# A fused attention and feed-forward layer in fp32: VectorE's sum of two probability tiles moved to another place in the unit, and GpSimd's work reordered

## What is computed

```python
xq = rope(q @ Wq); xk = rope(kv @ Wk); xv = kv @ Wv      # q = kv = layernorm(x)
xk = jnp.repeat(xk, 2, axis=-1); xv = jnp.repeat(xv, 2, axis=-1)
# 16 heads of 64
scores = jax.nn.softmax(xq @ xk * scale, axis=-1)
out = (scores @ xv) @ Wo
ffn = (silu(x @ w_gate.T) * (x @ w_up.T)) @ w_down.T     # x = layernorm(x) here too
x = x + out + ffn
```

## Time and profile before

| | us |
|---|---|
| median of three runs | 1159.65 (1156.83 to 1164.91) |
| the profiled execution | 1166.15 |
| its span, first to last instruction | 1164.4 |

### The profile page before, as it was taken

One profiled execution on the slowest core, in us unless ns is written; L12 is line 12 of the kernel. 1 busy time (PEld: TensorE's weight loads), 2 busy tenths in 40 slices (PEclk: granted clock), 3 DMA queues, 4 the chain that ended last, 5 costly groups with the idle time before them and its releaser, 6 DMA issues.

```text
span 1164.4 us, 17086 instructions
## 1 busy us (share of the span) xinstructions
PE 1120.0 (96%) x6288; PEld 663.2 (57%) x6288; DVE 901.1 (77%) x1023; ACT 729.8 (63%) x1327; POOL 852.9 (73%) x268
## 2 busy tenths in 40 slices
PE   5899899999999999999999999999999999999997
PEld 4787455655565555556565555555555555554443
DVE  7686877787887877788787877778787877776655
ACT  3234666666676666666676666666676666665564
POOL 3222868788788778888788778887778878887660
PEclk9899999999999999999999999999999999998889
DMA  6662908062340718062341718072341618050000
GB/s 230 159 258 77 256 2 224 1 205 58 85 141 19 207 37 224 2 205 57 96 129 26 201 37 224 1 210 53 96 130 30 196 37 224 1 130 1 5 1 19
DMA packets 56338, 124.98 MB, mean 107 GB/s; under 512 B 8000, under 2 KB 19520, under 8 KB 54080
## 3 DMA queue, kind: packets, MB, share of 16 engines
q1 hardware_dynamic: 56256, 123.90, 36.8%
HBM read 53.08 MB, written 10.49 MB: 55 GB/s over the span
## 4 chain that ended last, share of the span: by engine, by line
PE 79%; DVE 14%; SPq 2%; ACT 2%; issue 1%; DMA 1%; POOL 0%; DVEq 0%; ACTq 0%; POOLq 0%
PE bank_o L406 20%; PE bank_s L554 18%; PE scores L391 17%; DVE row_max L946 12%; PE scores L373 7%; PE bank_m L381 3%; PE bank_m L442 2%; PE bank_m L416 2%; PE bank_m L419 2%; SPq L239 2%; PE scores L492 2%; PE bank_s L509 1%; ACT prob L867 1%; PE bank_o L509 1%; DVE stats L961 1%
## 5 line engine op out<-in xcount | busy, mean ns | idle before, releaser
L946 DVE TENSOR_REDUCE row_max<-scores 128x1 f32<-128x1024 f32 x512 | 597.1, 1214 | 206.8 <-PE scores L391 206.5
L867 ACT ACTIVATE prob<-bank_s 128x512 f32<-128x512 f32 x992 | 576.7, 600 | 252.9 <-PE bank_s L554 229.5
L1181 POOL TENSOR_TENSOR prob_sum<-prob_sum,prob 128x2048 f32<-128x2048 f32 x93 | 425.7, 4577 | 13.5 <-ACT prob L867 0.5
L554 PE MATMUL bank_s<-qk_pack 98*128 98x512 f32 x992 | 415.8, 434 | 7.1 <-ACT prob L867 3.1
L391 PE MATMUL scores<-qk_pack 96*128 96x512 f32 x1024 | 337.5, 411 | 8.9 <-DVE row_max L946 0.3
L554 PEld LDWEIGHTS bank_s<-qk_pack 98*128 98x128 f32 x992 | 186.9, 189 | 184.9 <-issue 84.7
L406 PE MATMUL bank_o<-prob,v 128*32 128x512 f32 x2048 | 253.0, 612 | 0.0
L391 PEld LDWEIGHTS scores<-qk_pack 96*128 96x128 f32 x1024 | 179.5, 190 | 74.5 <-DVE row_max L946 53.0
L1181 POOL TENSOR_TENSOR prob_sum<-prob_sum,prob_pair 128x2048 f32<-128x2048 f32 x31 | 142.7, 4602 | 101.7 <-DVE prob_pair L1039 101.7
L1125 POOL TENSOR_TENSOR qk_stage<-rope,qk_stage 128x512 fp32r<-128x512 f32 x64 | 81.8, 1279 | 92.3 <-ACT qk_stage L753 92.3
L1173 POOL TENSOR_TENSOR prob_sum<-prob 128x2048 f32<-128x2048 f32 x31 | 142.2, 4586 | 0.0
(11 more groups left out here) (105 smaller groups left out, 742.4 us busy)
## 6 DMA issues: line engine op xcount, KB each, us to landing
qk_pack<-qk_stage SPq DMA_DIRECT2D x384, 128.0 KB, 5.0
table<-tables SPq DMA_DIRECT2D x16, 2048.0 KB, 9.6
w_stage<-w_scratch SPq DMA_DIRECT2D x14, 640.0 KB, 4.5
v<-v_stage SPq DMA_DIRECT2D x32, 256.0 KB, 8.1
xT_scratch<-xT_hl SPq DMA_DIRECT2D x4, 1024.0 KB, 9.5
x_stage<-xT_scratch SPq DMA_DIRECT2D x4, 1024.0 KB, 7.0
w_scratch<-w_split SPq DMA_DIRECT2D x1, 2560.0 KB, 15.1
x_all<-x SPq DMA_DIRECT2D x4, 512.0 KB, 11.7
```

Source lines behind the costliest of these rows:

```text
L554: mm(bank_s[:, h % 2, :], qk_pack[j][0:SCORE_K, 1, kt // QT, h, (kt % QT) * 128:(kt % QT + 1) * 128], qk_pack[j][0:SCORE_K, 0, t, h, :], s ...
L867: A(prob[:, kt % RING, h, :], bank_s[:, h % 2, :], ACT.Exp).then_inc(prob_ready, 1)
L946: V.tensor_reduce(row_max[:, m:m + 1], scores[:, at:at + 2, :].rearrange("p c k -> p (c k)"), axis=AX.X, op=ALU.max).then_inc(max_read, 1)
L1181: TT(prob_sum[:, t], prob_sum[:, t], part, ALU.add).then_inc(sum_done, 1)
```

## The change

DVE's `pair_sum(u)` now adds key tiles 2 and 3, and stands after maximum tile 11 (`PAIR_AFTER`), that is ahead of tiles 12 to 15, the split and the normalisation, where it stood behind them and ahead of `rotate`. GpSimd's order in a unit is now: first low part, add of 0+1, second low part, output add, then the pair (2+3), 4, 5 and 6. ACT's waits follow from the new readers of the ring: key tiles 6 and 7 wait for the pair, the next unit's key tiles 0, 1 and 2 for the adds of 4, 5 and 6. The arithmetic is the same but for the order of the sums. PE's and SyncE's streams are the same.

```diff
--- before.py
+++ after.py
@@ -70,6 +70,7 @@
 NE = HG
 
 INVERT_AFTER = 9
+PAIR_AFTER = 11
 
 
 def build(nc, x, tables, w_qkv, wo_even, wo_odd, w_gu, w_down, ident_in, out):
@@ -852,16 +853,14 @@
 
                     if not (first and kt < RING):
                         act.wait_ge(pv_done, 8 * u + kt - 3)
-                        if kt < 2:
-                            act.wait_ge(pair_done, u)
-                        elif kt == 2:
-                            act.wait_ge(sum_done, 5 * u)
+                        if kt < 3:
+                            act.wait_ge(sum_done, 5 * u - 2 + kt)
                         elif kt == 3:
                             act.wait_ge(den_ready, u)
                         elif kt < 6:
                             act.wait_ge(sum_done, 5 * u + 1)
                         else:
-                            act.wait_ge(sum_done, 5 * u + kt - 4)
+                            act.wait_ge(pair_done, u + 1)
                     for h in range(HG):
                         act.wait_ge(score_ready, 32 * u + 4 * kt + h + 1)
                         A(prob[:, kt % RING, h, :], bank_s[:, h % 2, :], ACT.Exp).then_inc(prob_ready, 1)
@@ -895,10 +894,8 @@
             def last_slot():
                 for kt in range(KT):
                     act.wait_ge(pv_done, 8 * LAST + kt - 3)
-                    if kt < 2:
-                        act.wait_ge(pair_done, LAST)
-                    elif kt == 2:
-                        act.wait_ge(sum_done, 5 * LAST)
+                    if kt < 3:
+                        act.wait_ge(sum_done, 5 * LAST - 2 + kt)
                     elif kt == 3:
                         act.wait_ge(den_ready, LAST)
                     elif kt < 6:
@@ -1034,9 +1031,9 @@
 
             def pair_sum(u):
 
-                dve.wait_ge(prob_ready, NE * (KT * u + 6))
-                at_least(dve, sum_done, 5 * u - 1)
-                V.tensor_tensor(prob_pair[:], prob[:, 4 % RING], prob[:, 5 % RING], ALU.add).then_inc(pair_done, 1)
+                dve.wait_ge(prob_ready, NE * (KT * u + 4))
+                at_least(dve, sum_done, 5 * u - 3)
+                V.tensor_tensor(prob_pair[:], prob[:, 2], prob[:, 3], ALU.add).then_inc(pair_done, 1)
 
             def invert(u):
                 dve.wait_ge(denT_ready, u + 1)
@@ -1056,12 +1053,14 @@
                         reduce_tile(u + 1, m)
                         if m == INVERT_AFTER and not is_first(u):
                             invert(u - 1)
+                        if m == PAIR_AFTER:
+                            pair_sum(u)
                     split_max(u + 1)
                 else:
                     invert(u - 1)
+                    pair_sum(u)
                 if not is_first(u):
                     normalise(u - 1)
-                pair_sum(u)
                 if not last_pair:
                     rotate(u + 4, t, 2 * i + j + 2)
 
@@ -1119,8 +1118,8 @@
         def _(pool):
             TT = nc.gpsimd.tensor_tensor
 
-            def split_lo(w, t):
-                for k in range(2):
+            def split_lo(w, t, halves=range(2)):
+                for k in halves:
                     pool.wait_ge(hi_done, 2 * w + k + 1)
                     TT(qk_stage[:, 2 * k + 1, t, :], rope[:, 2 * k, :], qk_stage[:, 2 * k, t, :].bitcast(F32), ALU.subtract).then_inc(lo_done, 1)
 
@@ -1166,18 +1165,21 @@
 
             pool.wait_ge(filled, 3)
 
-            def add_probs(u, t):
+            def add_first(u, t):
 
                 at_least(pool, den_ready, u - 1)
                 pool.wait_ge(prob_ready, NE * (KT * u + 2))
                 TT(prob_sum[:, t], prob[:, 0], prob[:, 1], ALU.add).then_inc(sum_done, 1)
-                for n, kt in enumerate((2, 3, 4, 6)):
-                    if kt == 4:
+
+            def add_rest(u, t):
+
+                for n, kt in enumerate((2, 4, 5, 6)):
+                    if kt == 2:
                         pool.wait_ge(pair_done, u + 1)
                     else:
                         pool.wait_ge(prob_ready, NE * (KT * u + kt + 1))
                     pool.wait_ge(sum_done, 5 * u + n + 1)
-                    part = prob_pair[:] if kt == 4 else prob[:, kt % RING]
+                    part = prob_pair[:] if kt == 2 else prob[:, kt % RING]
                     TT(prob_sum[:, t], prob_sum[:, t], part, ALU.add).then_inc(sum_done, 1)
 
             def add_out(u, t, b):
@@ -1190,11 +1192,15 @@
 
             def slot(i, j, t, last_pair):
                 u = 4 * i + 2 * j + t
-                if not (last_pair and (j, t) != (0, 0)):
-                    split_lo(u + 3, 1 - t)
+                staged = not (last_pair and (j, t) != (0, 0))
+                if staged:
+                    split_lo(u + 3, 1 - t, range(0, 1))
+                add_first(u, t)
+                if staged:
+                    split_lo(u + 3, 1 - t, range(1, 2))
                 if not is_second(u):
                     add_out(u - 2, t, (u - 2) // UNITS_B)
-                add_probs(u, t)
+                add_rest(u, t)
 
             def body(i, last_pair):
                 for j in range(2):
```

## The result

| | before | after |
|---|---|---|
| median of the runs, us | 1158.95 (1156.83 to 1164.91, 4 runs) | 1182.65 (1179.98 to 1185.25, 4 runs) |
| ratio, 95% interval | | 1.0204 (1.0161 to 1.0246) |
| the profiled execution, us | 1166.15 | 1182.11 |
| its span, us | 1164.4 | 1180.3 |
| busy share of the span: PE, DVE, POOL, ACT | 96, 77, 73, 63% | 96, 75, 72, 62% |

The change made the kernel 2.0% slower. The forecast was 1179 (1173 to 1290). The 23.7 us between the medians depend in part on the four runs of the kernel before: 28 later runs of the same kernel have a median of 1163.05 (1155.79 to 1166.32), which would leave 19.6.

The account below looks back on a forecast made before the run. It took PE, busy 96% of the span, to bound the kernel, losing time only in waits on DVE. 31 x 0.62 = 19.2 us on 1166.15 made 1185.4, on the median's base 1179 us, range 1173 to 1290.

Parts of the forecast that it names:

- The pair in its new place: On DVE ahead of tile 12: the 2.20 us pair exceeds the 1.58 us room, costing 0.62 us per unit; chance 0.55.
- The old place: At DVE's end of unit, ahead of `rotate`: the pair's 2.20 us leave, gain nothing, at most 0.2 us in the run.
- relief: Rival at the unit's end: PE really waits on DVE's `rotate`, so 49 us less, 1111; chance of faster 0.04.
- GpSimd's order, the low parts and the packs: GpSimd's adds and a low part 3.7 us later stay covered, zero cost; rival of late packs 1234, chance 0.04.
- The lock: DVE's low part may stand still behind GpSimd's add of tile 4: 1288 to 1340; chance 0.20 all units, 0.13 some.
- the clock: On PE after a stall from the lost race: clock granted at 0.50 for a while, adding up to 1.67 us.
- ACT has no wait on GpSimd: Sign of being right: ACT's new waits for adds of tiles 4, 5, 6 are covered by 2.7, 2.5 and 1.0 us.

Follow-up runs that it names:

- the short reduction: The kernel before plus an unread VectorE reduction of a 128x1408 constant after maximum tile 11: 1162.02 us, ratio 1.0004.
- The three kernels with moved maximum tiles: The kernel before with PE's tile 12 between V products of tiles 2 and 3, tile 7 ahead of denominators, or both: 1173.56, 1174.21, 1185.71 us.
- The long reduction: The kernel before plus an unread VectorE reduction of a 128x2048 constant after maximum tile 11: 1177.98 us, ratio 1.0147.
- the delayed one: The changed kernel with an unread 128x128 VectorE reduction ahead of the cast and low part of the maxima: 1343.52 us, ratio 1.1576.
- GpSimd's old order: The changed kernel with GpSimd doing both low parts, the output add, then the add of 0+1, as before: 1181.48 us, ratio 1.0185.
- the guard: GpSimd's add of tile 4 waits for the low part of the maxima: 1181.67 us on the changed kernel, 1182.02 with the added reduction ahead of the cast.
- the control: The changed kernel with an unread 128x128 VectorE reduction behind the low part of the maxima: 1181.11 us, ratio 1.0164.

## Why the prediction was right, and where it missed

- **The pair in its new place: right.** It took 2.20 us, stood straight behind tile 11, and a unit grew by 0.59 us against the forecast 0.62 (a hole of 1.58). The two inserted reductions show the bound itself: 1.59 us cost 0.00 in a unit, 2.20 cost 0.61. Over the 27 intervals it is 15.6 us; over 31 units it would be 18.4, against the forecast 19.2.
- **The old place: right.** Nothing was gained there. DVE idles at `rotate` now, for 33.6 us in 30 units; the rival "relief" would have needed PE to wait for DVE there.
- **GpSimd's order, the low parts and the packs: right in the steady units.** ACT shows no wait on GpSimd there, and undoing the order changes nothing that can be measured.
- **The lock: the numbers were right, the outcome was open.** The forecast put the cast 6.85 us after the pair's start, the low part at 7.06 and the add of tile 4 at 7.08. Measured, as medians over the units: 6.85, 7.05 and 7.08. The rows of before didn't say whether so small a lead suffices; the changed kernel shows that it does, in 31 units of 31. The forecast price of losing it, 1288 to 1340, was met at its upper end, or a little above (1343.52 for the kernel that loses it): the clock, which I carried as an "or", is part of the price each time, and in one unit of three it was 3.0 us where the forecast allowed 1.67.
- **"ACT has no wait on GpSimd": wrong in the last unit**, and this step had no term in the sum. The last unit has neither projections nor maximum tiles between its scores, and ACT's places in the ring now need the single adds of tiles 4, 5 and 6 of the unit before, where its key tiles 0 and 1 needed the pair only. GpSimd works these off one after another. ACT's timeline, and pieces of the chain in that part:

```profile
1142.84 1.09 ACT L908 ACTIVATE prob<-scores 128x512 f32<-128x512 f32 x2 [1.44 <-POOL prob_sum L1183]
...
1147.54 0.60 ACT L908 ACTIVATE prob<-scores 128x512 f32<-128x512 f32 x1 [1.15 <-POOL prob_sum L1183]
```

```profile
1126.50 2.21 DVE prob_pair L1036
...
1133.50 4.59 POOL prob_sum L1183
...
1138.22 4.55 POOL prob_sum L1183
...
1142.93 4.53 POOL prob_sum L1183
```

  ACT waited 2.6 us for GpSimd, and the chain runs through its adds. The part from the last transposition to the end is 45.7 us, against 43.6 before. It is tempting to put these 2.1 us down to the change, but the other kernels don't bear that out. With the pair of tiles 4 and 5 in its old place, the kernel with the short reduction has such a wait too, and its last part is 45.1 us:

```profile
1128.56 0.60 ACT L912 ACTIVATE prob<-scores 128x512 f32<-128x512 f32 x1 [2.32 <-POOL prob_sum L1189]
```

  The three kernels with moved maximum tiles have it as well (2.3 us, with a last part of about 45). The long reduction has none (43.0). Among the kernels that sum tiles 2 and 3 the part is 45.5 to 46.0, but 44.4 in the delayed one. So the changed kernel may lose a microsecond or two here; no run separates that from how an execution happens to end.
- **Unit 1: not foreseen.** In the profiled execution of before PE waited 2.45 us for V's DMA and its clock fell; that interval was 36.53 us, and 33.07 after. The forecast carried this stall over to the changed kernel. The DMA was issued at 137.22 us before and at 136.18 after, but in the short-hole kernel the wait was there too (2.52 us), in the long-hole one 1.45, and with GpSimd's old order none. Five other kernels without the wait spent 31.5 to 32.5 us in the interval ahead of it, at a granted clock of 0.84, where the kernel before spent 28.14 at 1.00. What sets either is not settled.

The two ends of the run differ between profiled executions by more than the change moves them. The first two intervals together took 61.7 to 65.6 us and the last two 61.0 to 68.7, over the eleven kernels other than the delayed one and the one with the pair after tile 13. The last two were 68.7 and 68.2 in the changed kernel and in the same one with the guard, at a granted clock of 0.90, and 62.6 in the control at 1.00; the steady intervals of these three agree within 0.02. One kernel varies alike: the quickest run of the kernel before took 1155.79 us at a mean granted clock of 0.993, the slowest 1166.32 at 0.983. The steady part is where the change can be read, and there it costs 0.59 to 0.61 us in a unit, 18 to 19 us in 31. The four kernels with the changed kernel's steady interval (GpSimd's old order, the control and the two with the guard) ended 18.1 to 19.0 us above the kernel before beside them, close to the forecast 19.2. The rest of the 23.7 in the first comparison is no more than what the ends of the runs vary by.

The prediction was carried by one term, and that term was read from one row: the idle time of DVE ahead of tile 12. That the race of the low part went its way was not known beforehand: the sum left the lock out, the prediction gave 0.33 to its being lost in all or in some units, and the outcome hung on 0.01 to 0.03 us. To that extent the number is luck.

## What to carry to other kernels

Before work is moved into a hole of an engine, measure the hole and the work from start to start: what fits is free, and what is longer goes on the path in every unit, even if it leaves a busy place elsewhere. Where VectorE has an instruction with two SBUF inputs, or a small cast, near the start of a long GpSimd instruction, write the order down with a wait: it cost nothing here, and it stands between 1182 and 1343 us. Read the steady units apart from the first and the last ones: here the last two intervals alone differed by 6 us between kernels whose steady units were the same.

## What the runs showed of the hardware that I had not expected

- A recorded lead of 0.01 to 0.03 us between starts was enough for VectorE's low part in 31 units of 31; 0.03 to 0.06 us behind, it lost in all 31 units of the delayed kernel and stood for 4.53 us. This is no general rule: the tensor_scalar of the earlier trace rows had a recorded lead of 0.04 us and ended with GpSimd's add all the same. The outcome repeated from unit to unit: the runs of the delayed kernel lie within 1343.39 to 1345.58.
- Waits of 3.2 to 3.3 us on TensorE cost 1.6 us more through the granted clock with the pair after tile 13, and 2.1 on average in the delayed kernel (1.7, 1.7, 3.0 in turn), so that these stalls had a price half to two thirds as high again as their length.
- Breaking a group of 16 V products (128 by 32 columns of weights) once with two full-width matmuls cost 0.34 us. The Trainium skill, page "TensorEngine Tiling (Array Packing)", section "Key Properties", says that changing the tiling mode drains TensorE; it gives no figure. The 0.34 us agree with such a rule in sign, but no run here separates it from other causes.
